# A selective scan with two PSUM banks for its inputs' products and one summing product per channel group

## The chip, the cores and the metric

The kernel runs on one core of a Trainium2 chip. A core has five engines that work side by side and meet at semaphores: PE (matrix products into PSUM), DVE (vector), ACT (activations), POOL (GpSimd) and SP, which here only issues DMAs. [...] The metric is the time of one execution on the device in microseconds.

## The reference

The input is x of shape (8, 512, 128): 8 sequences of 512 positions with 128 channels. Six layers are added to x in turn: an adapter FFN, attention, the same FFN, a mixture of experts, the selective scan, the same mixture. Only the scan layer is touched. It gets xn, the layer norm of x, and computes per sequence

```
u     = silu(conv3(xn))                    # depthwise, three taps along the positions
B, C  = split(u @ W_bc + b_bc)             # 16 numbers each per position
dt    = log1p(exp((u @ W_dt + b_dt) @ W_dtp + b_dtp))
alpha = exp(A * dt)                        # per channel d and state n, A = -exp(A_log)
beta  = B[n] * xn[d] * dt[d]
h[l]  = alpha[l] * h[l-1] + beta[l]        # the scan along the positions
y[d]  = sum over n of C[n] * h[d, n] + xn[d] * Dcoeff[d]
```

and x becomes x + y. 128 channels with 16 states each are 2048 recurrences of 512 steps.

## The kernel before

All of x stays in SBUF. The scan layer treats the sequences one after the other. The 2048 recurrences of one sequence are 16 groups of 8 channels x 16 states = 128 partitions, 512 positions in the free dimension.

Work is laid out by hand in steps and slots. A step (`over_steps`) treats three sequences at a time: `new`, whose dt, B and C are being made, `old`, whose 16 groups are scanned, and `older`, whose y is added to X; `ahead` is `new + 1`, whose convolution and projections are made. A step has 16 slots, `n` = 0 to 15. Each engine runs its own list of these slots in order, and within a slot in the order of the lines. An engine that waits for a semaphore holds up all that stands behind it on that engine.

For group m of `old` the work is:

- SP loads the 8 rows of dt, each 16 times, from DRAM into a ring buffer `dtb` (`load_dt`, L1598, 256 KB). It waits until ACT has used that buffer before. DT_RING is 4.
- ACT makes alpha from it in PSUM (`pA`, L1848). A_RING is 3: the write waits until scan m - 3 is over.
- PE spreads x * dt over the states from `stack` (three bf16 parts that add up to the value) into `pX` (`spread_xdt`, L1709), two slots ahead, in three banks.
- DVE multiplies pX with B into `beta` (L1891) and, one slot later, runs the scan into `h` (L1874).
- POOL multiplies h with C into `hc` (L1662), a ring of 8.
- PE sums over the states: `add_round` (L1724) takes four groups at a time in slots 6, 10, 14 and, for the last four, in slot 1 of the next step. Group 4r + t goes with a 32-column weight to PSUM partitions 32t to 32t + 31 of `pY`, into which the skip term x * D was written first (`skip_term`, L1717, four products of 32 columns). ACT copies the finished pY to yT (L1854).

The inputs of a sequence pass on PE through one PSUM bank `z`. `event` (L1671 to L1700) issues seven kinds of products into it: b and c (B and C spread over partitions, L1699, slots 2 and 3), y (four transposes back to rows, L1693, slot 4), xT (four transposes, L1682, slot 7), u (the convolution as three products with diagonal weights, L1686, slot 9), bc (two projections, L1689 and L1690, slot 12), lin (dt's second projection, L1696, slot 14). Each waits for its own input and until the one before it was read out of z. The readers are ACT, for b (L1828), c (L1831), xT (L1793), exp of u (L1796), the bias additions (L1804, L1805) and exp of dt (L1810), and DVE, for y (the addition to X, L1883, slot 5) and u (the product with 1/(1 + exp(-u)), called inv, L1868, slot 11).

dt and x * dt are then finished by ACT and POOL: w and its logarithm, nd, corr, dt, xdt (POOL L1631 to L1643, slots 1, 3, 4, 5), the three bf16 parts (ACT L1836 and L1839, POOL L1646 and L1649, slots 6 to 8). SP writes dt to DRAM in slot 6 and copies the parts into the stack in slot 10, 12 DMAs one after the other (L1590) once the third part is there; only then follow the next sequence's loads of dt.

PSUM has eight banks: pA 3, pX 3, pY 1, z 1.

Of the kernel before, what the change touches and what calls it, by code (L numbers as in the profile page):

```python
# [14 lines left out]
ALU = mybir.AluOpType  # L15
# [5 lines left out]
P = 128  # L21
# [1418 lines left out]
A_RING = 3  # L1440
X_RING = 3
DT_RING = 4
B_RING = 4
HC_RING = 8
LOW = 64
PARTS = 3
# [70 lines left out]
def selective_scan(nc, g, q, sem, tag):  # L1517
# [5 lines left out]
        "c_ready", "xdt_bcast", "alpha_ready", "beta", "h_ready", "hc_ready", "rounds", "y_taken", "y_done", "x_done",  # L1523
# [4 lines left out]
    with ExitStack() as ctx:  # L1528
# [9 lines left out]
        xT = [sb(f"xT{i}", [P, L + 2]) for i in range(2)]  # L1538
# [16 lines left out]
        z = ps("z", [P, L])  # L1555
        z3 = z[:, :].rearrange("p (c d) -> p c d", c=NC)
# [22 lines left out]
        def _(sp):  # L1579
# [4 lines left out]
            def stack_parts(b):  # L1584
                sp.wait_ge(s.split, b + 1)
                if b > 1:
                    sp.wait_ge(s.xdt_bcast, NS * (b - 1))
                for part in range(PARTS):
                    for t in range(TILES):
                        sp.dma_start(stack[b % 2][32 * part:32 * part + 32, t, :], parts[32 * t:32 * t + 32, part, :]  # L1590
                                     ).then_inc(stack_in[b % 2], 16)

            def load_dt(b, n):
                if n == 0:
                    sp.wait_ge(s.dt_out, 16 * (b + 1))
                wait_for(sp, s.alpha_ready, NS * b + n - DT_RING)
                first = channels(n)
                sp.dma_start(dtb[n % DT_RING][:, :],  # L1598
                             dt_dram[b % 2, first:first + DG, :].unsqueeze(1).broadcast_to([DG, NS, L])
                             ).then_inc(dt_in[n % DT_RING], 16)  # L1600

            def step(new, old, older):
                for n in range(NS):
                    if new is not None and n == 6:
                        write_dt(new)
                    if new is not None and n == 10:
                        stack_parts(new)
# [3 lines left out]
                    elif new is not None:  # L1611
                        load_dt(new, n + DT_RING - NS)

# [3 lines left out]
        def _(pool):  # L1617
            def zero_columns():
                pool.memset(xT[0][:, :], 0.0)
                pool.memset(xT[1][:, :], 0.0).then_inc(s.zeros_made, 1)  # L1620
# [7 lines left out]
            def inputs(b, n):  # L1628
# [3 lines left out]
                if n == 3:  # L1632
# [3 lines left out]
                if n == 4:  # L1636
# [4 lines left out]
                if n == 5:  # L1641
                    pool.wait_ge(s.dt_ready, b + 1)
                    pool.tensor_tensor(xdt[:, :], xT[b % 2][:, 1:L + 1], dt[:, :], ALU.mult).then_inc(s.xdt_ready, 1)  # L1643
# [7 lines left out]
            def step(new, old, older):  # L1651
                for n in range(NS):
                    if new is not None:
                        inputs(new, n)
                    if old is not None:
# [4 lines left out]
                        if m >= HC_RING:  # L1660
                            pool.wait_ge(s.rounds, m // TILES - 1)
# [6 lines left out]
        def _(pe):  # L1668
            pe.wait_ge(s.zeros_made, 1)

            def event(name, b, last):  # L1671

                need = {"xT": s.xn_ready, "u": s.xT_ready, "bc": s.us_ready, "lin": s.bc_ready, "b": s.bc_ready,
# [296 lines left out]
```

## Time and profile before

| | us |
|---|---|
| median of 3 executions | 1702.7 (1701.62 to 1707.16) |
| the profiled execution | 1707.51 |
| its span, first to last instruction | 1705.8 |
| PE busy in it | 1428.3 (84%) |
| DVE busy | 962.8 (56%) |
| ACT busy | 776.0 (45%) |
| POOL busy | 376.1 (22%) |

The profile's lines belong to one execution. An engine is busy while one of its instructions runs; matrix products are pipelined, so a busy PE is not PE at its peak. "Idle before" is the time that an engine stood still ahead of an instruction, and the arrow names what it waited for last. The scan layer runs from about 1016 us (its first instruction) to 1382 us, a little over a fifth of the span, and the shares above say little of it; windows and timelines of that stretch are read instead.

### The profile page before, as it was taken

Reading aid. Unit: us, or ns where it says so; the run is one execution under the profiler, and the core shown is the slowest. Engines: PE = TensorE matmul, PEld = TensorE weight load, DVE = VectorE, ACT = ScalarE, POOL = GpSimd, SP = SyncE. Lnnn points to the kernel's source line nnn. Section 1 sums busy time; section 2 is a strip of 40 time slices with the busy share of each in tenths; the row PEclk is TensorE's granted clock in tenths of the full one; section 3 lists DMA queues with packets and bytes.
Section 4 is the critical chain, followed back from the end, with each engine's and each line's share of the span. In section 5 each row is a group of like instructions: output and inputs, shape, how many; then the busy total and the mean of one; then the engine's idle time right before and its main releaser. Section 6 shows DMA issues by size and latency. Waiting matters only on the chain. (4 is left out here: it accounts for less than half of the span.)

```text
span 1705.8 us, 23654 instructions
## 1 busy us (share of the span) xinstructions
PE 1428.3 (84%) x7538; PEld 771.7 (45%) x7538; DVE 962.8 (56%) x1959; ACT 776.0 (45%) x1362; POOL 376.1 (22%) x475
## 2 busy tenths in 40 slices
PE   3983899999999688699999965777777559999998
PEld 2661223233322366567776741111111037777776
DVE  4663788888888166441222460777677864122235
ACT  0210488888888421154334323645554314433342
POOL 2004232321230100120000011666666630000000
PEclk9995799999999799599999986666766558999999
DMA  4002121222220000100000000433333410000001
GB/s 85 1 1 74 47 70 45 66 66 75 67 74 21 1 1 1 16 15 15 1 15 15 1 1 26 141 123 119 122 125 121 118 36 15 3 13 15 15 7 44
DMA packets 80052, 77.28 MB, mean 45 GB/s; under 512 B 19468, under 2 KB 59224, under 8 KB 79960
## 3 DMA queue, kind: packets, MB, share of 16 engines
q1 hardware_dynamic: 77840, 75.85, 14.6%
q8 instruction: 49, 0.80, 0.2%
q10 hardware_dynamic: 2120, 0.28, 0.1%
q14 instruction: 43, 0.35, 0.1%
HBM read 55.78 MB, written 16.78 MB: 43 GB/s over the span
## 5 line engine op out<-in xcount | busy, mean ns | idle before, releaser
L1258 ACT ACTIVATE m_hidden<-m_pU,m_up_b 128x512 f32<-128x512 f32 x320 | 219.9, 687 | 271.8 <-PE m_pU L1395 271.5
L1013 DVE TENSOR_REDUCE at_nm<-at_mx 128x2 f32<-128x1024 f32 x256 | 303.1, 1221 | 45.6 <-PE at_mx L857 44.3
L1402 PEld LDWEIGHTS m_pD<-m_down,m_hidden 128*128 128x128 f32 x2560 | 296.9, 192 | 33.5 <-issue 33.5
L1402 PE MATMUL m_pD<-m_down,m_hidden 128*128 128x128 f32 x2560 | 297.1, 275 | 0.0
L1395 PE MATMUL m_pU<-m_xT_all,m_up 128*128 128x512 f32 x640 | 291.3, 601 | 1.1 <-PEq L1094 1.1
L959 ACT ACTIVATE at_probs<-at_ring 128x512 f32<-128x512 f32 x512 | 268.3, 601 | 45.4 <-PE at_ring L869 44.6
L1371 DVE TENSOR_TENSOR m_out_b<-m_pD,m_down_b 128x512 f32<-128x512 f32 x64 | 44.2, 691 | 283.8 <-PE m_pD L1402 283.8
L1662 POOL TENSOR_TENSOR ss_hc<-ss_h,ss_c_all 128x512 f32<-128x512 f32 x128 | 161.0, 1267 | 113.2 <-DVE ss_h L1874 106.1
L857 PE MATMUL at_mx<-at_kk,at_qq 48*128 48x512 bf16 x512 | 158.3, 399 | 23.6 <-DMA at_kk<-k_stack 13.2
L1395 PEld LDWEIGHTS m_pU<-m_xT_all,m_up 128*128 128x128 f32 x640 | 118.0, 193 | 123.8 <-issue 123.5
L869 PE MATMUL at_ring<-at_qq,at_kk 51*128 51x512 bf16 x512 | 166.6, 386 | 8.0 <-ACT at_probs L959 4.9
L1874 DVE TENSOR_TENSOR_SCAN ss_h<-ss_pA,ss_beta 128x512 f32<-128x512 f32 x128 | 154.8, 1214 | 11.0 <-issue 4.4
L881 PE MATMUL at_po<-at_probs,at_va 128*32 128x512 f32 x1024 | 136.9, 607 | 0.1
L122 POOL TENSOR_TENSOR rstd<-ln_u,neghalf 128x4 f32<-128x4 f32 x6 | 6.1, 1023 | 552.2 <-DVE ln_u L114 552.2
L1709 PE MATMUL ss_pX<-ss_stack,ss_spread 96*128 96x512 bf16 x128 | 64.8, 522 | 67.4 <-DVE ss_beta L1891 62.1
L1848 ACT ACTIVATE ss_pA<-ss_dtb,ss_a_neg 128x512 f32<-128x512 f32 x128 | 87.1, 685 | 47.0 <-DMA ss_dtb<-ss_dt_rows 34.7
L857 PEld LDWEIGHTS at_mx<-at_kk,at_qq 48*128 48x128 bf16 x512 | 34.4, 95 | 131.7 <-DVE at_nm L1013 76.2
L1891 DVE TENSOR_TENSOR ss_beta<-ss_pX,ss_b_all 128x512 f32<-128x512 f32 x128 | 85.0, 669 | 5.9 <-PE ss_pX L1709 5.9
L1709 PEld LDWEIGHTS ss_pX<-ss_stack,ss_spread 96*128 96x128 bf16 x128 | 13.0, 106 | 161.8 <-DVE ss_beta L1891 113.6
L1377 DVE SCALAR_TENSOR_TENSOR m_acc<-m_out_b,m_w_listed,m_acc 128x128 f32<-128x128 f32 x256 | 73.2, 347 | 9.3 <-DVE m_out_b L1371 2.4
L869 PEld LDWEIGHTS at_ring<-at_qq,at_kk 51*128 51x128 bf16 x512 | 36.5, 93 | 63.7 <-ACT at_probs L959 42.3
L347 PE MATMUL f_pG<-f_hx 128*128 128x257 f32 x256 | 60.1, 387 | 5.2 <-ACT f_hx L386 5.2
(244 smaller groups left out, 1588.7 us busy)
## 6 DMA issues: line engine op xcount, KB each, us to landing
ss_dtb<-ss_dt_rows SPq DMA_DIRECT2D x128, 256.0 KB
at_qq<-q_stack SPq DMA_DIRECT2D x64, 96.0 KB, 2.3
at_kk<-k_stack SPq DMA_DIRECT2D x64, 96.0 KB, 2.3
q_stack<-at_qs SPq DMA_DIRECT2D x8, 384.0 KB, 2.6
k_stack<-at_ks SPq DMA_DIRECT2D x8, 384.0 KB, 3.0
ss_stack<-ss_parts SPq DMA_DIRECT2D x96, 32.0 KB, 1.9
X<-in_L_attn_x_dram SPq DMA_DIRECT2D x8, 256.0 KB, 5.6
q_stack<-at_qs SPq DMA_DIRECT2D x8, 256.0 KB, 2.9
```

The costliest lines, as they stand in the source:

```text
L857: last = pe.matmul(mx[parity][:, c, :], qq[rows(parity, STACK), pair, q_at:q_at + P], kk[rows(parity, STACK), pair, :], start=True, stop=True)
L869: pe.matmul(ring[bank][:, :], kk[rows(h, STACK + 3), h // 2, tile * P:(tile + 1) * P], qq[rows(h, STACK + 3), h // 2, :], start=True, stop ...
L881: last = pe.matmul(po[VW * h4:VW * (h4 + 1), :], va[:, tile, group * GH + h4, :], probs[:, (slot % 2) * GH + h4, :], start=(tile == 0), st ...
L959: act.activation(probs[:, (slot % 2) * GH + ORDER[j], :], ring[bank][:, :], ACT.Exp, scale=SCALE).then_inc(s.exp_done, 1)
L1013: dve.tensor_reduce(nm[group % 2][:, 2 * half:2 * half + 2, 2 * (pair % 2) + parity], mx[parity][:, :, :], AX.X, ALU.max, negate=True).the ...
L1258: act.activation(hidden[t % 2][:, k, :], pU[k][:, :], ACT.Gelu, bias=up_b[buf][:, k:k + 1]).then_inc(s.gelu_done, 1)
L1395: pe.matmul(pU[k][:, :], up[buf][:, k * P:(k + 1) * P], xT_all[:, t, :], start=True, stop=True).then_inc(s.up_done, 1)
L1402: last = pe.matmul(pD[t % 2][:, c, :], hidden[t % 2][:, k, c * P:(c + 1) * P], down[buf][:, k, :], start=(k == 0), stop=(k == NI - 1))
L1662: pool.tensor_tensor(hc[m % HC_RING][:, :], h[m % HC_RING][:, :], c_all[old % 2][:, :], ALU.mult).then_inc(s.hc_ready, 1)
L1848: act.activation(pA[m % A_RING][:, :], dtb[n % DT_RING][:, :], ACT.Exp, scale=a_neg[:, column:column + 1]).then_inc(s.alpha_ready, 1)
L1874: dve.tensor_tensor_scan(h[m % HC_RING][:, :], pA[m % A_RING][:, :], beta[m % B_RING][:, :], 0.0, ALU.mult, ALU.add).then_inc(s.h_ready, 1)
L1891: dve.tensor_tensor(beta[m % B_RING][:, :], pX[m % X_RING][:, :], b_all[old % 2][:, :], ALU.mult).then_inc(s.beta, 1)
```

## The change

- The bank z becomes two: `zx` holds xT and the convolution, `zy` holds y, b, c, the two projections and dt's second projection. pA gives up a bank for it: A_RING 3 to 2.
- `event` is replaced by functions with their own waits, and the slots are dealt out anew. On PE: xT of `ahead` in slot 1 (was 7), the convolution one product each in slots 3, 4, 5 (was 9), y in slot 4, b in 7 (was 2), c in 9 (was 3), the projections in 11 (was 12), lin in 13 (was 14). ACT, POOL, DVE and SP follow: the addition to X in slot 7 (was 5), the product with inv in 10 (was 11), POOL's corr, dt, xdt one slot earlier, the normalisation of x a step earlier and in two halves (slots 11 and 13).
- `add_round` becomes `add_group`: each group's states are summed by a product of its own, three slots after the group's place (groups 0, 1, 2 together in slot 5, 13, 14, 15 in slots 0, 1, 2 of the next step). `hc` buffers come free one by one.
- xT has three buffers instead of two, cleared by one memset more. dtb has six instead of four.
- SP writes dt in slot 4 (was 6), and the stack is copied in three parts in slots 7, 9 and 11, each as soon as its bf16 part is there (was all in slot 10).

```
-A_RING = 3
+A_RING = 2
-DT_RING = 4
+DT_RING = 6
+X_SEQS = 3
...
-        z = ps("z", [P, L])
+        zx, zy = ps("zx", [P, L]), ps("zy", [P, L])
...
-                    if new is not None and n == 6:
-                        write_dt(new)
-                    if new is not None and n == 10:
-                        stack_parts(new)
...
+                    if new is not None and n == 4:
+                        write_dt(new)
+                    if new is not None and n in (7, 9, 11):
+                        stack_part(new, (n - 7) // 2)
...
-                            pool.wait_ge(s.rounds, m // TILES - 1)
+                            pool.wait_ge(s.summed, m - HC_RING + 1)
...
+            def transpose_x(b):
+                pe.wait_ge(s.xn_ready, b + 1)
+                if b > 0:
+                    pe.wait_ge(s.us_ready, b)
...
+            def y_rows(b):
+                pe.wait_ge(s.y_taken, b + 1)
+                pe.wait_ge(s.e_dt, min(b + 3, NB))
...
+            def spread_b(b):
+                if b > 1:
+                    pe.wait_ge(s.x_done, b - 1)
+                pe.wait_ge(s.e_dt, b + 1)
...
+            def spread_c(b):
+                pe.wait_ge(s.b_ready, b + 1)
...
+            def project(b):
+                pe.wait_ge(s.us_ready, b + 1)
+                if b > 0:
+                    pe.wait_ge(s.c_ready, b)
...
-            def add_round(b, r):
-                wait_for(pe, s.hc_ready, NS * b + TILES * r + TILES - 1)
-                first = (ROUNDS - 1 - r) * DG
-                for t in range(TILES):
-                    ins = pe.matmul(pY[32 * t:32 * t + 32, :], q.total[:, first:first + 32],
-                                    hc[(TILES * r + t) % HC_RING][:, :], start=False, stop=(r == ROUNDS - 1),
-                                    skip_group_check=True)
-                ins.then_inc(s.rounds, 1)
+            def add_group(b, n):
+                wait_for(pe, s.hc_ready, NS * b + n)
+                tile = n % TILES
+                first = (ROUNDS - 1 - n // TILES) * DG
+                pe.matmul(pY[32 * tile:32 * tile + 32, :], q.total[:, first:first + 32], hc[(NS * b + n) % HC_RING][:, :],
+                          start=False, stop=(n // TILES == ROUNDS - 1), skip_group_check=True).then_inc(s.summed, 1)
...
+                    if n == 1 and ahead is not None:
+                        transpose_x(ahead)
+                    if n < 3 and older is not None:
+                        add_group(older, NS - 3 + n)
+                    if n in (3, 4, 5) and ahead is not None:
+                        convolve(ahead, n - 3)
                     if n == 4 and old is not None:
                         skip_term(old)
                     if n == 4 and older is not None:
+                        y_rows(older)
+                    if n > 4 and old is not None:
+                        for group in range(0 if n == 5 else n - 3, n - 2):
+                            add_group(old, group)
+                    if n == 7 and new is not None:
+                        spread_b(new)
+                    if n == 9 and new is not None:
+                        spread_c(new)
+                    if n == 11 and ahead is not None:
+                        project(ahead)
+                    if n == 13 and ahead is not None:
+                        lift(ahead)
```

ACT's list has the matching order: the copy of xT in slot 2, of pY in 3, the cast of xdt in 5, exp of the convolution in 6, the cast of rest and the logarithm in 7, inv in 8, the copies of b and c in 9 and 10, the bias additions in 12, exp of dt in 14, w in 15.

## Rows read from the trace of the kernel before

**Rows 1.** The page's part 2, 40 slices of the span.

```profile
PE   3983899999999688699999965777777559999998
...
PEclk9995799999999799599999986666766558999999
```

**Rows 2.** Windows from first scan to next; us, busy by engine, clock, DMA share, GB/s.

```profile
1068.70:1105.00 36.30, 26.49 (x68) 6.36 (x67) 28.23 (x33) 20.78 (x37) 26.58 (x22) 0.69 0.39 133
1105.00:1145.80 40.80, 30.21 (x80) 7.67 (x80) 29.86 (x40) 21.91 (x40) 27.06 (x23) 0.67 0.36 122
...
1346.80:1375.50 28.70, 16.40 (x57) 2.88 (x56) 27.88 (x37) 10.89 (x16) 18.98 (x16) 0.56 0.44 124
sum 306.80, PE 212.29 PEld 51.24 DVE 234.68 ACT 150.15 POOL 207.95; mean PE 26.54 PEld 6.40 DVE 29.34 ACT 18.77 POOL 25.99
```

**Rows 3.** Groups by line, 1030 to 1390; busy us, mean ns, idle before, releaser.

```profile
L1662 POOL TENSOR_TENSOR ss_hc<-ss_h,ss_c_all 128x512 f32<-128x512 f32 x128 | 161.0, 1267 | 113.2 <-DVE ss_h L1874 106.1 <-issue 7.0
L1874 DVE TENSOR_TENSOR_SCAN ss_h<-ss_pA,ss_beta 128x512 f32<-128x512 f32 x128 | 154.8, 1214 | 11.0 <-issue 4.4 <-DVE ss_beta L1891 3.6 <-ACT ss_pA L1848 2.9
...
L1891 DVE TENSOR_TENSOR ss_beta<-ss_pX,ss_b_all 128x512 f32<-128x512 f32 x128 | 85.0, 669 | 5.9 <-PE ss_pX L1709 5.9
...
L96 DVE BATCH_NORM_STATS2 bn<-X 128x6 f32<-128x128 f32 x32 | 6.9, 279 | 0.0
```

**Rows 4.** Timeline 1186.5 to 1200.5; start, us, engine, line, idle before and releaser.

```profile
1192.26 2.04 PE L1699 MATMUL ss_z<-ss_bc,ss_pick_bc 32*128 32x512 f32 x2 [0.23 <-ACT ss_b_all L1828]
...
1194.77 1.94 PE L1717 MATMUL ss_pY<-ss_xT,ss_diag_d 128*32 128x512 f32 x8
...
1196.63 0.93 PE L1693 MATMUL ss_z<-identf,ss_yT 128*128 128x128 f32 x4
...
1197.61 0.69 DVE L1883 TENSOR_TENSOR X<-X,ss_z 128x512 f32<-128x512 f32 x1 [4.65 <-PE ss_z L1693]
```

**Rows 5.** Timeline 1200 to 1219, what stands before the us product.

```profile
1203.59 0.62 ACT L1836 CAST ss_parts<-ss_xdt 128x512 bf16<-128x512 f32 x1 [5.93 <-POOL ss_xdt L1643]
...
1207.80 4.36 PE L1686 MATMUL ss_z<-ss_xT,ss_diag_k 128*128 128x512 f32 x6 [2.14 <-ACT ss_xT L1793]
...
1209.48 7.53 SPq L1590 DMA_DIRECT2D ss_stack<-ss_parts  x12
...
1212.19 0.60 ACT L1796 ACTIVATE ss_e<-ss_z 128x512 f32<-128x512 f32 x1 [3.34 <-PE ss_z L1686]
...
1214.61 0.69 DVE L1868 TENSOR_TENSOR ss_us<-ss_z,ss_inv 128x512 f32<-128x512 f32 x1 [4.45 <-ACT ss_inv L1801]
```

**Rows 6.** The same stretch, PE's products at full clock.

```profile
1211.99 0.38 PE L1709 MATMUL ss_pX<-ss_stack,ss_spread 96*128 96x512 bf16 x1
...
1212.30 1.07 PE L1724 MATMUL ss_pY<-ss_hc,ss_total 128*32 128x512 f32 x8
...
1213.30 0.39 PE L1709 MATMUL ss_pX<-ss_stack,ss_spread 96*128 96x512 bf16 x1
...
1216.28 1.04 PE L1689 MATMUL ss_z<-ss_us,ss_w_bc 128*32 128x512 f32 x2
```

**Rows 7.** Timeline 1022 to 1076, a 32-column product at half clock.

```profile
1061.16 1.89 PE L1689 MATMUL ss_z<-ss_us,ss_w_bc 128*32 128x512 f32 x2 [2.83 <-DVE ss_us L1868]
```

**Rows 8.** Windows of clock and DMA within the scan.

```profile
1187.10:1197.00 9.90, 9.67 (x25) 1.99 (x26) 5.85 (x7) 6.92 (x15) 8.62 (x7) 0.50 0.41 138
1197.20:1200.60 3.40, 1.27 (x9) 0.45 (x11) 2.96 (x8) 0.45 (x1) 0.00 (x0) 0.99 0.60 192
1200.70:1210.40 9.70, 6.30 (x18) 2.25 (x11) 8.94 (x11) 4.13 (x7) 9.34 (x8) 0.50 0.20 65
...
1220.00:1230.00 10.00, 6.93 (x24) 1.55 (x24) 10.00 (x13) 7.27 (x12) 7.70 (x8) 0.73 0.52 195
1348.00:1368.00 20.00, 12.81 (x47) 2.37 (x39) 19.19 (x27) 8.12 (x12) 13.06 (x11) 0.59 0.53 148
```

**Rows 9.** Timeline 1009 to 1024.5, the start of the scan.

```profile
1018.01 0.53 POOL L1620 MEMSET ss_xT<- 128x514 f32 x1
```

More of the change, by code:

```diff
@@ L1537, in selective_scan @@
         xn = sb("xn", [P, NC, D])
-        xT = [sb(f"xT{i}", [P, L + 2]) for i in range(2)]
+        xT = [sb(f"xT{i}", [P, L + 2]) for i in range(X_SEQS)]
         dt, xdt, rest = sb("dt", [P, L]), sb("xdt", [P, L]), sb("rest", [P, L])
@@ L1618, in zero_columns @@
             def zero_columns():
-                pool.memset(xT[0][:, :], 0.0)
-                pool.memset(xT[1][:, :], 0.0).then_inc(s.zeros_made, 1)
+                for i in range(X_SEQS):
+                    last = pool.memset(xT[i][:, :], 0.0)
+                last.then_inc(s.zeros_made, 1)
             take_rstd(pool, g, s.var, s.rstd, zero_columns)
@@ L1772, in _, with norm @@
             act.wait_ge(s.zeros_made, 1)
-            def norm(b):
-                act.wait_ge(s.rstd, NB)
-                act.wait_ge(s.shift, 2)
-                if b > 0:
-                    act.wait_ge(s.xT_done, b)
-                for c in range(NC):
+            def norm(b, half):
+                if half == 0:
+                    act.wait_ge(s.rstd, NB)
+                    act.wait_ge(s.shift, 2)
+                    if b > 0:
+                        act.wait_ge(s.xT_done, b)
+                for c in (2 * half, 2 * half + 1):
@@ L1851, in step @@
                         back(new, n)
-                    if n == 2 and older is not None:
-                        act.wait_ge(s.rounds, ROUNDS * older + ROUNDS)
+                    if n == 3 and older is not None:
+                        act.wait_ge(s.summed, NS * older + NS)
                         act.copy(yT[:, :], pY[:, :]).then_inc(s.y_taken, 1)
-                    if following(new) is not None:
-                        front(new + 1, n)
+                    if ahead is not None:
+                        front(ahead, n)
+                    if following(ahead) is not None and n in (11, 13):
+                        norm(ahead + 1, (n - 11) // 2)
+            for half in range(2):
+                norm(0, half)
             for n in range(NS):
+                if n == 4:
+                    for half in range(2):
+                        norm(1, half)
                 front(0, n)
```

181 lines of the change are left out of this document (79 added, 102 removed).

## The prediction, made before the changed kernel ran

> **What bounds the kernel now.** I read the page's slices first [rows 1]: the change touches only the scan, the stretch from about 1026 to 1382 us, and there the granted clock of TensorE sinks to 0.5 to 0.7 while PE is busy for 6 to 7 tenths. Then the windows from one sequence's first scan to the next one's [rows 2]. Eight of them make 306.8 us: 36.3, then six that make 241.8 (40.3 each), then 28.7 for the last sequence. In a middle one (40.8 us) DVE is busy for 29.86, POOL for 27.06, PE for 30.21 at a clock of 0.67, ACT for 21.91. No engine is full, so each waits for another in turn.
>
> The groups by line [rows 3] give the pieces: per channel group DVE does one product of 0.67 and one scan of 1.21 us, which overlap a little. 29.86 less the us product (0.69), the add to X (0.69) and the statistics (0.86 and a small copy) leaves 27.5, or 1.72 per group. POOL does 22 operations of about 1.26 per sequence, 27.1 busy. The floors are 29.8 (DVE) and 27.1 (POOL).
>
> What DVE waits for is seen in the order of time. One wait is the add to X [rows 4]: idle 4.65 us until the transposes of y into z are done. These stand in PE's order behind b, its copy, c, its copy and the skip term: all of them use the one bank z or stand between its users, and all run at half clock (2.04 for c, 1.94 for the skip term). The other is the us product [rows 5]: idle 4.45 until ACT has made inv. ACT sat 5.93 us before its cast of xdt (POOL's xdt comes late because POOL itself stood still while DVE waited for X), so it copied xT late, the three products of the convolution ran 1207.80 to 1212.16, and e, e1, inv followed. The two waits are 9.1 of the interval's 10 idle us. Both are latency in a chain, not a full engine.
>
> **The change part by part.** I count in slots, one per group, and in warm (full) clock unless said.
>
> *Two banks and the new places.* y's transposes now go to zy in slot 4 and the add to X stands in slot 7, three slots later (5 us). xT's transposes move from slot 7 to slot 1, the convolution from 9 to 3 to 5, e, e1, inv to 6, 7, 8, and the us product stands in slot 10. The b and c products move behind them (7 and 9). So the 4.65 and the 4.45 both go, if PE reaches slot 4 and 5 in time. Removed idle: 9.1 per middle interval at most, which would give 31.
>
> *Sum per group instead of rounds.* In [rows 6] a round, four products on 32 columns each, is issued as 8 passes and takes 1212.30 to 1213.30, 1.00 us for all four: they run side by side. A single product on 32 columns of the same 512 (L1689) takes 1.04 with its tail, so alone each costs what the round costs. Between any two of the new group products stands a spread product on all 128 columns, so they can't run together. Twelve products of 1.0 are added: +12 us of PE per sequence. A slot costs 0.31 (spread, 1211.99 to 1212.30) + 1.00 = 1.31.
> PE per sequence is then 16 x 1.31 = 21.0, the skip term 1.0, convolution 2.7 (half of what it takes cold, about 5.3), b and c 2.0, the two projections 2.0, dt 1.0, the two sets of transposes 1.0: 30.7 us warm. At half clock (one 32-column product 1.89 [rows 7], the rest doubled) it is about 58.
> [...]
>
> *Which clock.* [Rows 8]: PE was busy for 9.67 of 9.90 us at 0.50, and the next 3.4 us were granted 0.99; in these PE was busy for 1.27 only, and behind them stands 0.50 again. In [rows 1] the slices with PE at 9 have a clock of 9. With 30.7 of work in about 31.5, PE has no idle stretch of more than a microsecond, so I take full clock for the middle intervals. This is the largest choice in the forecast and is priced below.
>
> *The walk through one middle interval.* With the DVE slots at 0, 0.6, 2.3, 4.0, 5.7, 7.5, 9.2, 10.9, then the add to X, PE runs slots 0 to 3 by 5.5; slot 4 (spread, convolution, skip term, y) ends at 8.2, so y is there before DVE's slot 7 at 10.9: this wait is gone. Slot 5 (spread, convolution, three group sums) ends at 12.4, which DVE doesn't feel, since its next two spread products are already issued (three pX banks).
> POOL: hc of group 0 at 2.3, then nd, corr, dt, xdt between the hc's, xdt done at 12.2, rest at 15.8, the third part at 19.5.
> ACT is the tight one, since pA has two banks instead of three: the exponential of group n may begin only when scan n-2 is over, and is wanted 2.3 us later, 0.69 of them its own; so anything that ACT waits for behind exponential n has about 0.9 us to spare after slot n+1 has begun. Its cast of xdt in slot 5 comes at 12.2 and delays scan 6 by 0.5 (most of it is under the add to X). The cast of rest in slot 7 comes at 15.8 and delays scan 8 by 0.75. c's product waits for the copy of b and PE idles about 1 us there. The bias copies in slot 12 wait for the projections (25.3) and delay scan 13 by 0.55. dt in slot 14 just fits. Sum: 29.5 + 2.0 = 31.5, and PE arrives at the end of the same interval at 31.4. Queue overheads that I didn't walk: I add 0.5 and take 32.
> Bounds of the interval: 29.8 (DVE alone) and, if each of the four late handovers to ACT comes 1 us later, 35.5.
>
> *DMA.* Per sequence 16 loads of 256 KB, 12 of 32 KB and the 256 KB written, 4.85 MB. [Rows 8] show 195 GB/s in one dense stretch and 148 in the last sequence, at the same share (0.52, 0.53): 24.9 or 32.8 us. SP's own issuing is 12 in 7.53 us [rows 5] for the stack and about 0.6 for each load: 17.5 per sequence, so it is not full. On SP the write of dt now waits with loads 11 onward queued behind it, until POOL's dt at 9.7; six buffers instead of four cover that (load 11 is wanted at 21). The stack goes in three fours, the last behind loads for the next sequence, and lands near 28 for a use at 28.8: small margin, up to 1 us if missed.
>
> *The ends.* The third xT buffer is cleared on POOL between the two parts of rstd, for which ACT's first normalisation waits: 0.5 us [rows 9]. The step that fills the pipe keeps its chain at half clock; b and c stand later, the stack starts earlier: 0, within 2 either way. The interval of sequence 0 has neither y nor X: 30. That of sequence 6 has no convolution behind it: 30. The last sequence has DVE at 27.88 of 28.70 already [rows 2] and stays 28.7; after it the last sum is one product instead of four at the same time: 0.
> Sum: 30 + 5 x 32 + 30 + 28.7 = 248.7 against 306.8, and 0.5 for the memset: 57.6 us less. The profiled execution took 1707.5 us for a span of 1705.8 and would become 1649.9. It stands 4.8 above the median of the three runs shown, 1702.7, so I forecast 1645 for the median.
>
> **The rivals.**
> *The clock stays where it is (slower).* Mechanism: PE's waits for hc and for banks keep it from looking busy, the clock stays at 0.67 as in the middle intervals [rows 2], and PE now has 12 us more to do. A third of the time warm and two thirds cold gives 1/(0.34/30.7 + 0.66/58) = 44.5 per interval; with 30 for the last, 341 against 307: 35 us more, 1738. It decides below a mean granted clock of 0.75, where the interval is 40.3 as before. For it: PE was busy through 9.9 us before the clock rose [rows 8], and the low clock of the whole stage. Against: an engine with 12 us more work has no room for idle stretches like the one before that fall. [...]
> *ACT becomes the bound, through two pA banks.* 35.5 per middle interval and 33 for the two beside: 5 x 35.5 + 66 + 28.7 = 272, 35 less: 1668. For it: in the walk every remaining stall is of this kind. Against: after DVE's own delay ACT has caught up.
> *The loads.* At 148 GB/s throughout, 33 per interval: 7 x 33 + 30 = 261, 46 less: 1657. For it: the last sequence ran so from end to end. Against: dense stretches before it had 195.
> *The waits are not removed* because the two banks are held as long as the one was (zy still takes y, b, c, both projections and dt): the intervals stay near 39 and PE's extra work is hidden: 1697 to 1703, no change.
>
> **How the numbers follow.** Forecast with its own spread (1635 to 1652) 0.55; loads 0.12; ACT 0.18; no change 0.04; clock 0.08; better than the walk, to DVE's floor (28.2 + 5 x 29.8 + 29.4 + 27.9 = 234.5, 1630), 0.03. The range 1634 to 1670 leaves out the clock, no change and a little of the rest. A difference of 0.3% (5 us) is what a measurement of this kernel can tell from none. Faster 0.88, same 0.04, slower 0.08.
>
> **What would show it.** Right: from scan to scan 31 to 33 us, DVE busy over 90% of it, no wait of DVE for the transposes or inv over 1 us, PE's granted clock above 0.95 in the middle intervals, PE busy for over 28 us of each, single group sums about 1 us apart from their spread product. ACT's exponentials then wait for scans. Wrong: a clock below 0.75 there; or DVE's scans waiting for pA by several us per interval behind ACT's casts or bias copies; or ACT's exponentials waiting for dtb at a steady 1.77 us.

## The result, and the profile after

| | before | after |
|---|---|---|
| median | 1703.5 us (1701.62 to 1707.16, 4 executions) | 1642.34 us (1639.34 to 1647.64, 4 executions) |
| the profiled execution | 1707.51 | 1639.34 |
| its span | 1705.8 | 1637.6 |
| granted clock of TensorE, mean (1 is full speed) | 0.870 | 0.932 |

The ratio is 0.9642, 95% interval 0.9608 to 0.9676: the change makes the kernel 61 us faster. 1645 had been forecast, with a range of 1634 to 1670. The profiled execution of the kernel before is not one of the four in its median.

The page's slices of the span show where it happened; the rows answer to [rows 1].

```profile
PE   3893799999999869689999995699998769999998
PEclk9996699999999989769999998689999959999999
```

In the scan PE now stands at 9 in slices 27 to 30, and its clock at 8 or 9 in slices 27 to 32, where both had 5 to 7.

The same windows as [rows 2], from a sequence's first scan to the next one's (the first, three middle ones, the last, and the sum of all eight):

```profile
1061.80:1093.40 31.60, 28.18 (x66) 6.13 (x65) 28.48 (x34) 21.60 (x39) 27.08 (x22) 0.82 0.50 154
1093.40:1124.60 31.20, 30.19 (x84) 7.04 (x83) 30.01 (x41) 20.29 (x36) 26.90 (x22) 0.98 0.48 161
...
1156.20:1188.90 32.70, 30.52 (x82) 6.98 (x80) 29.93 (x40) 20.75 (x37) 27.02 (x23) 0.95 0.50 151
1188.90:1220.10 31.20, 27.39 (x79) 6.61 (x78) 29.93 (x41) 20.78 (x37) 27.12 (x23) 1.00 0.47 150
...
1281.10:1309.00 27.90, 22.21 (x61) 3.94 (x60) 27.82 (x37) 10.17 (x15) 19.17 (x16) 0.98 0.30 107
sum 247.20, PE 221.39 PEld 49.13 DVE 235.08 ACT 147.99 POOL 208.43; mean PE 27.67 PEld 6.14 DVE 29.39 ACT 18.50 POOL 26.05
```

The usual middle interval takes 31.2 us and not 40.8. DVE's work is what it was (29.93 against 29.86), so what went is its idle time, from 11 to 1.3 us. The waits of DVE in one middle interval, before (first fence) and after (second), show the same. The columns are: what waited for what, us in total, times, longest.

```profile
DVE ss_us L1868 <- ACT ss_inv L1801: 5.6, 1, 5.6
DVE X L1883 <- PE ss_z L1693: 4.8, 1, 4.8
DVE ss_h L1874 <- DVE ss_beta L1891: 0.5, 1, 0.5
```

```profile
DVE ss_h L1899 <- DVE ss_beta L1916: 1.2, 2, 1.0
```

Both named waits are gone and nothing of weight stands in their place. Lines from the timelines of PE, DVE and ACT in a middle interval, with the places of [rows 4 to 6]:

```profile
1188.06 1.05 PE L1739 MATMUL ss_pY<-ss_hc,ss_total 128*32 128x512 f32 x2
...
1189.03 0.39 PE L1724 MATMUL ss_pX<-ss_stack,ss_spread 96*128 96x512 bf16 x1
...
1196.99 1.06 PE L1739 MATMUL ss_pY<-ss_hc,ss_total 128*32 128x512 f32 x6
...
1198.62 0.66 DVE L1908 TENSOR_TENSOR X<-X,ss_zy 128x512 f32<-128x512 f32 x1
...
1200.16 0.62 ACT L1847 CAST ss_parts<-ss_xdt 128x512 bf16<-128x512 f32 x1 [4.10 <-POOL ss_xdt L1645]
...
1201.83 1.22 DVE L1899 TENSOR_TENSOR_SCAN ss_h<-ss_pA,ss_beta 128x512 f32<-128x512 f32 x1 [1.00 <-DVE ss_beta L1916]
...
1206.68 0.67 DVE L1893 TENSOR_TENSOR ss_us<-ss_zx,ss_inv 128x512 f32<-128x512 f32 x1
1207.15 1.12 PE L1704 MATMUL ss_zy<-ss_bc,ss_pick_bc 32*128 32x512 f32 x2 [1.05 <-ACT ss_b_all L1853]
...
1217.46 0.39 PE L1724 MATMUL ss_pX<-ss_stack,ss_spread 96*128 96x512 bf16 x1 [1.09 <-DMA ss_stack<-ss_parts]
```

The addition to X (1198.62) and the product with inv (1206.68) follow their predecessors at once. Most of the idle time that DVE has left stands at 1201.83: ACT sat 4.10 us before its cast of xdt, so the exponential behind it was late. The profile names beta there, which had ended a microsecond before; in new_xdt_early below, where the cast comes earlier, the wait is gone. c's product waits 1.05 for the copy of b and runs warm, which is to say at full clock (1.12 us at a granted 1.00; cold, at a granted 0.50, it took 2.04 in [rows 4]). The line at 1196.99 holds three group sums, x6 being two passes for each: with no spread product between them they took 1.06 us together.

The profiled spans differ by 68.2 us: 59.6 in the eight intervals (306.8 to 247.2), 3.5 in the step that fills the pipe, 1.35 between the last scan and the next layer's rstd, 0.3 behind the layer, and 3.4 ahead of it, in layers that the change doesn't touch.

### The profile page after: what moved, and what is told of

It reads as the page before. It is cut to its first block and busy times, and to the rows that moved or that the text cites. A ratio compares the mean times of both kernels' runs of the same rounds, so it can differ in the third digit from the quotient of the medians.

```text
span 1637.6 us, 23647 instructions
## 1 busy us (share of the span) xinstructions
PE 1433.1 (88%) x7538; PEld 767.2 (47%) x7538; DVE 962.8 (59%) x1959; ACT 775.8 (47%) x1362; POOL 377.0 (23%) x476
## 5 line engine op out<-in xcount | busy, mean ns | idle before, releaser
L1664 POOL TENSOR_TENSOR ss_hc<-ss_h,ss_c_all 128x512 f32<-128x512 f32 x128 | 161.9, 1271 | 50.6 <-DVE ss_h L1899 40.8
L1739 PE MATMUL ss_pY<-ss_hc,ss_total 128*32 128x512 f32 x256 | 122.5, 622 | 11.7 <-POOL ss_hc L1664 11.6
L857 PEld LDWEIGHTS at_mx<-at_kk,at_qq 48*128 48x128 bf16 x512 | 34.3, 95 | 131.4 <-DVE at_nm L1013 77.7
L869 PEld LDWEIGHTS at_ring<-at_qq,at_kk 51*128 51x128 bf16 x512 | 36.5, 93 | 64.1 <-ACT at_probs L959 42.4
```

What stands on the lines that cost most here:

```text
L857: last = pe.matmul(mx[parity][:, c, :], qq[rows(parity, STACK), pair, q_at:q_at + P], kk[rows(parity, STACK), pair, :], start=True, stop=True)
L869: pe.matmul(ring[bank][:, :], kk[rows(h, STACK + 3), h // 2, tile * P:(tile + 1) * P], qq[rows(h, STACK + 3), h // 2, :], start=True, stop ...
L1664: pool.tensor_tensor(hc[m % HC_RING][:, :], h[m % HC_RING][:, :], c_all[old % 2][:, :], ALU.mult).then_inc(s.hc_ready, 1)
L1739: pe.matmul(pY[32 * tile:32 * tile + 32, :], q.total[:, first:first + 32], hc[(NS * b + n) % HC_RING][:, :], start=False, stop=(n // TILES ...
```

## The experiments

The times are medians, and each ratio is to the kernel before on the same chip. Beside the experiments that kernel took 1706.5, 1707.0 and 1705.1 us, beside the new one 1703.5, so where two changed kernels are compared the difference of their ratios is the fairer measure. "Intervals" are the eight from first scan to first scan in the profiled execution; the kernels' line numbers shift by a few.

**The rounds of four in the new kernel** (new_rounds), the last of them in slot 2 of the next step.

```
...
-                    if n > 4 and old is not None:
-                        for group in range(0 if n == 5 else n - 3, n - 2):
-                            add_group(old, group)
+                    if n in (6, 10, 14) and old is not None:
+                        add_round(old, (n - 6) // 4)
...
```

> The changed kernel with only the summing put back: rounds of four products side by side in slots 6, 10, 14 and in slot 2 of the next step. Theory of places (the gain comes from where y and the convolution stand, in two banks; the group products cost 12 us of PE that nothing waits for): DVE still does not wait for y or inv, 31 to 33 us per middle interval, 1638 to 1650 us, while the granted clock sinks to 0.6 to 0.8 because PE has 12 us less to do. Theory of the clock (the group products are what makes it fast, since they keep PE at full clock): the interval goes back to 34 to 37 us, 1662 to 1685. Theory of PE's load (PE at 30 of 31 us is what bounds the interval now): 30 us per interval, 1630 to 1634.

Measured: 1659.05 (1658.71 to 1661.37), 0.9723 (0.9706 to 0.9739). This lies between the forecasts of the three theories. The group products are worth 17 of the 61 us by the medians and 14 by the ratios, with some 6 us of uncertainty. The page's clock alone doesn't say how; PE's timeline in a middle interval does, with one line of DVE's at its end:

```profile
1146.94 0.39 PE L1724 MATMUL ss_pX<-ss_stack,ss_spread 96*128 96x512 bf16 x1 [1.61 <-DVE ss_beta L1917]
...
1150.77 2.07 PE L1704 MATMUL ss_zy<-ss_bc,ss_pick_bc 32*128 32x512 f32 x2 [3.44 <-ACT ss_b_all L1854]
...
1153.31 1.94 PE L1739 MATMUL ss_pY<-ss_hc,ss_total 128*32 128x512 f32 x8
...
1155.71 1.92 PE L1711 MATMUL ss_zy<-ss_us,ss_w_bc 128*32 128x512 f32 x2
1157.56 1.75 PE L1712 MATMUL ss_zy<-ss_us,ss_w_dt 128*64 128x512 f32 x2
1159.25 0.61 PE L1724 MATMUL ss_pX<-ss_stack,ss_spread 96*128 96x512 bf16 x2
...
1159.68 0.69 DVE L1917 TENSOR_TENSOR ss_beta<-ss_pX,ss_b_all 128x512 f32<-128x512 f32 x1 [1.85 <-PE ss_pX L1724]
```

With no group sums to do, PE stands idle for 1.61 and 3.44 us while it waits for beta and for b's copy. Behind the second gap c's product, the round and the two projections run at half clock (granted 0.50, 0.50 and 0.53), 7.7 us for what takes about 4.3 warm, an estimate from the warm times in these traces (1.12, 1.06, 1.04 and 1.07). The spread product behind them is late: DVE's beta waits 1.85 us for it at 1159.68. The interval is 34.0, with a clock of 0.80. POOL never waited for a sum here, so hc buffers that come free one by one are not what the group products bring.

**A product per group in the old kernel** (old_groups): one bank and its own slots, with `add_group` in slots 5 to 15 and 0, 1, and POOL and ACT waiting for single groups.

```
...
-                    if n in (6, 10, 14) and old is not None:
-                        add_round(old, (n - 6) // 4)
+                    if n > 4 and old is not None:
+                        for group in range(0 if n == 5 else n - 3, n - 2):
+                            add_group(old, group)
...
```

> The kernel before with only the summing changed: a product per group, three slots behind the group, bank z and all other slots as before. Theory of places: the two waits of DVE stay, only shorter by what the full clock takes off the b, c, skip and convolution products before them (about 2 us at each): 36 to 38 us per middle interval, clock 0.85 to 1, 1672 to 1688. Theory of the clock: the whole gain is here, 32 to 33 us, 1645 to 1655. A third, that 12 us more on PE cost time in the old order: 42 or more, 1715 or more.

Measured: 1690.54 (1685.17 to 1694.88), 0.9903 (0.9874 to 0.9933), 2.5 above the range of the theory of places and nearest to it. PE's sums stand in 13 places per sequence instead of 4 (groups 0 to 2 and groups 14 and 15 stand together), 1.04 us each at full clock, and the old kernel is 16 us faster. Its clock rises to 0.91 to 0.96 in the middle intervals, the waits shrink (y 2.3 to 4.4, inv 3.3), and the intervals go to 36.5 to 39.0.

**Two banks in the old kernel** (old_two_banks): A_RING 2, zx for xT and u, zy for the rest, each product waiting for the last reader of its own bank, all slots as before.

```
...
                 pe.wait_ge(need, b + 1)
-                if last is not None:
+                z, z3, bank = (zx, zx3, 0) if name in ("xT", "u") else (zy, zy3, 1)
+                if last[bank] is not None:
...
```

> The kernel before with only the banks changed: xT and the convolution in one bank, the rest in another, pA with two banks, all slots and the rounds of four as before. Theory of places: y still stands behind b, its copy, c, its copy and the skip term, and inv behind ACT's cast of xdt; both waits stay at 4 to 5 us, 39 to 41 us per interval, 1695 to 1712. Theory of the banks (what DVE waited for was the single bank): both waits shrink, 34 to 36 us, 1655 to 1675.

Measured: 1705.78 (1701.89 to 1709.5, 10 executions), 0.9991 (0.9979 to 1.0004): nothing. DVE's waits in a middle interval:

```profile
DVE ss_us L1870 <- ACT ss_inv L1803: 5.4, 1, 5.4
DVE X L1885 <- PE ss_zy L1694: 4.8, 1, 4.8
```

They stand where they stood, as the theory of places had it. In the old slots the one bank is not what the products waited for, and giving up the third pA bank has no cost that shows.

**The old kernel with PE kept busy** (old_filled): each spread product issued four times over, nothing else.

```
+FILL = 4
...
-                pe.matmul(pX[m % X_RING][:, :], q.spread[:, n // TILES, :, :].rearrange("c d n -> c (d n)"),
...
+                for k in range(FILL):
+                    ins = pe.matmul(pX[m % X_RING][:, :], q.spread[:, n // TILES, :, :].rearrange("c d n -> c (d n)"),
...
```

> The kernel before with each spread product issued four times into the same bank instead of once (same result, 11 us more of PE per sequence at full clock, no new wait). It has the clock's part alone. Theory of places: clock 0.85 to 1, the two waits 2 to 3 us each instead of 4.5 to 5, 36 to 38 us per middle interval, 1672 to 1690. Theory of the clock: 32 to 34, 1645 to 1658. If the added products cost more than the clock gives back: over 1705.

Measured: 1685.17 (1680.0 to 1686.3), 0.9862 (0.984 to 0.9883). Work that nobody needs makes this kernel 21 us faster, at least as much as the group sums do. First a window of 36 us that runs from this kernel's second interval into its third, then the third interval of the kernel with the group products:

```profile
1105.00:1141.00 36.00, 30.20 (x127) 9.74 (x127) 29.16 (x39) 20.80 (x36) 26.40 (x22) 0.95 0.39 135
```

```profile
1142.00:1178.50 36.50, 29.22 (x81) 6.91 (x81) 30.00 (x40) 21.54 (x38) 27.07 (x23) 0.95 0.39 136
```

Both show a clock of 0.95 where [rows 2] have 0.67. The middle intervals of the filled kernel have 0.91 to 0.95 and take 36.7 to 39.8 us. The other thing that group sums could bring, hc buffers that come free one by one, nobody waited for: in [rows 3] POOL's idle time before hc is 106.1 us for scans and 7.0 of issue, none for a sum. So in the old kernel the group sums act as filling.

**The same filling in the new kernel with rounds** (new_rounds_filled).

> The changed kernel with rounds of four put back and each spread product issued four times: the group products' effect on the clock without the group products. If they help by the clock alone (theory): the granted clock is back at 0.95 or more, the intervals are 31 to 32 us and the time 1637 to 1646, as with the group products. If their own merit counts (each sum follows its hc at once, hc buffers come free one by one): it stays at 33.5 to 34, near 1655 to 1660.

Measured: 1663.4 (1661.05 to 1663.73), 0.9753 (0.9737 to 0.9769), slower than either forecast. The mean clock rose from 0.80 to 0.90 and the time did not fall (1659 without it), so a better mean clock is not by itself what the group products bring. PE's timeline shows where the filling missed:

```profile
1146.38 1.92 PE L1726 MATMUL ss_pX<-ss_stack,ss_spread 96*128 96x512 bf16 x8
1151.10 2.07 PE L1705 MATMUL ss_zy<-ss_bc,ss_pick_bc 32*128 32x512 f32 x2 [2.81 <-ACT ss_b_all L1857]
1153.11 1.89 PE L1726 MATMUL ss_pX<-ss_stack,ss_spread 96*128 96x512 bf16 x4
1154.92 1.94 PE L1742 MATMUL ss_pY<-ss_hc,ss_total 128*32 128x512 f32 x8
```

The gap before c's product is still 2.81 us, and half clock stands behind it, now with the filling to do as well. DVE's wait for pX is 2.4 to 2.7 us per middle interval, where it was 1.7 to 1.9 without the filling.

**Only the gap filled** (new_rounds_gap_filled): the spread products of slots 8 and 9 issued 8 and 11 times, the others once.

```
...
+                for k in range({10: 8, 11: 11}.get(n, 1)):
...
```

> The new kernel with the sums in rounds of four again, and two of the sixteen spread products issued 8 and 11 times over (slots 8 and 9), just ahead of c's product. With the rounds alone (1659) PE stood idle for 3.44 us there, waiting for b's copy, and then ran c's product (2.07), the round (1.94) and the projections (1.92, 1.75) at half clock. Filling the spread products all over the interval did not help (1663), but it left 2.8 us of idle in just this place and half clock behind it. Theory 'the sums per group matter because they fill this one gap': c's product, the round and the projections run at full clock, DVE's waits for pX (1.9 per interval) go to under 0.5, intervals about 31.5 to 32.5 us and the time 1640 to 1649. Rival 'rounds are late in themselves, since each waits for its fourth group and stands ahead of the spread products': the intervals stay near 34 and the time at 1657 to 1663.

Measured: 1649.95 (1644.6 to 1652.03), 0.9684 (0.9665 to 0.9704), 1 us above what the first theory gave and well below the rival's 1657. The window of one middle interval, DVE's waits in it, and PE behind the gap:

```profile
1124.00:1155.70 31.70, 27.14 (x99) 7.48 (x98) 29.73 (x40) 20.72 (x37) 27.01 (x23) 0.82 0.46 154
```

```profile
DVE ss_h L1902 <- DVE ss_beta L1919: 1.9, 3, 0.7
```

```profile
1142.23 1.12 PE L1704 MATMUL ss_zy<-ss_bc,ss_pick_bc 32*128 32x512 f32 x2 [1.29 <-ACT ss_b_all L1856]
...
1143.60 1.09 PE L1741 MATMUL ss_pY<-ss_hc,ss_total 128*32 128x512 f32 x8
...
1145.17 1.92 PE L1711 MATMUL ss_zy<-ss_us,ss_w_bc 128*32 128x512 f32 x2
```

c's product and the round are warm, the wait for pX is gone, and the interval is 31.7 at a mean clock of 0.82, lower than the 0.90 of the kernel that needed 34.3. So this one gap is worth about half of what the group products are: 9 of the 17 us by the medians, 7 of the 14 by the ratios, with some 4 us of uncertainty. The theory's full clock at the projections did not come (1.92). The other half is not taken apart: besides the cold projections, DVE waits 0.7 to 1.8 us for pX in the last three intervals (32.6, 31.8, 28.9 against 31.2, 29.8, 27.9 after).

**The addition to X two slots later in the old kernel** (old_late_add), one bank and rounds as before.

```
-                    if n == 5 and older is not None:
+                    if n == 7 and older is not None:
```

> The kernel before with DVE's addition to X in slot 7 instead of 5, nothing else. Theory of places, for the single bank: the wait for y shrinks by two slots (3.4 us), but the transposes of xT wait for that addition in the one bank and inv comes no earlier, so the wait for inv grows by as much: 1698 to 1710, no change. If each wait stood for itself: 3.4 us less per interval, 1680 to 1686.

Measured: 1673.42 (1672.31 to 1676.6), 0.9814 (0.9796 to 0.9833): half of the whole gain from one digit. My theory, no change, fell, and the time is 7 us below the lowest that independent waits gave. The window, DVE's waits, and the timeline of the same interval:

```profile
1138.24:1172.59 34.35, 24.43 (x81) 6.31 (x80) 30.13 (x40) 20.78 (x37) 27.16 (x23) 0.80 0.42 137
```

```profile
DVE ss_us L1868 <- ACT ss_inv L1801: 2.4, 1, 2.4
DVE X L1883 <- PE ss_z L1693: 1.0, 1, 1.0
```

```profile
1149.42 1.27 POOL L1643 TENSOR_TENSOR ss_xdt<-ss_xT,ss_dt 128x512 f32<-128x512 f32 x1
...
1150.72 0.62 ACT L1836 CAST ss_parts<-ss_xdt 128x512 bf16<-128x512 f32 x1 [1.52 <-POOL ss_xdt L1643]
...
1154.23 0.58 ACT L1793 COPY ss_xT<-ss_z 128x512 f32<-128x512 f32 x1
...
1154.95 2.81 PE L1686 MATMUL ss_z<-ss_xT,ss_diag_k 128*128 128x512 f32 x6 [1.21 <-ACT ss_xT L1793]
```

The wait for y falls from 4.8 to 1.0, as it would. But the wait for inv, which stood six slots behind the addition and now stands four, falls too, from 5.6 to 2.4 (to 2.4 in three of the middle intervals, to 3.9 and 4.2 in the others). In [rows 5] ACT sat 5.93 us before its cast of xdt; here it sits 1.52. While DVE waited for y it made no h, so POOL stood before its next hc with xdt queued behind, ACT stood before the cast with xT's copy queued behind, and PE's convolution was late and at least partly cold (4.36 there, granted 0.50 and then 0.83; 2.81 here, granted 1.00). So about 2 of the 5 us of the second wait came from the first, by the mean over the middle intervals.

**Both in one bank** (old_groups_late_add).

> The kernel before (one bank z, its own slots) with two changes alone: a product per group, and the addition to X in slot 7 and not 5. Apart they gave 1690.5 and 1673.4 against 1706. Theory: each takes part of the same waits (y: 4.7, and 2.3 to 4.4 with the group products; inv: 5.6, to 2.4 with the late addition and 3.3 with the group products), so together y goes to 0.5 or less and inv to 1 to 2.4; intervals 33 to 34.5, time 1656 to 1668. If that holds, more than half of the change's gain needs no second bank. Rival 'they add up in full': 1655 to 1659. Rival 'the late addition has it all': 1671 to 1675.

Measured: 1671.53 (1667.87 to 1675.31), 0.9814 (0.9791 to 0.9838), the same as with the late addition alone: the rival "the late addition has it all" was right. My own theory, 1656 to 1668, fell. The wait for y is gone in four of the intervals 2 to 6 and 1.0 in the other one, the third. The wait for inv stays at 3.3 to 3.4 (4.9 in the third), and the intervals take 34.2 to 34.8 (35.9):

```profile
DVE ss_us L1868 <- ACT ss_inv L1801: 3.3, 1, 3.3
```

So half of the gain needs neither the second bank nor the group products. What is left is the wait for inv, and the new slots start the convolution earlier. No run has these slots with one bank, and as they are laid out they need two: zx is held from the convolution in slot 3 until the product with inv in slot 10, and y, b and c pass through zy meanwhile.

**The addition to X back in slot 5 of the new kernel** (new_add_early).

> The new kernel with the addition to X back in slot 5. By the walk y's transposes end about 8.2 us after the first beta, and DVE's slot 5 begins at 7.5 to 9: the wait for y would be 0 to 1 us, and since the old kernel showed that a wait of DVE there is passed on to POOL and ACT, up to 2 us more. Theory 'with the two banks y is early and the place of the addition is nearly free': intervals 31 to 32.5, 1641 to 1651. Rival 'the place of the addition is what counts in the new kernel too': intervals 33 and more, 1655 or more.

Measured: 1647.66 (1641.3 to 1649.65), 0.9655 (0.9625 to 0.9684), 5 us above the new kernel by the medians and 2 by the ratios, whose intervals overlap: as the first theory had it. The waits for y are 0.7 to 0.8 in four of the middle intervals, and these take 31.2 to 32.8 as without the edit. The other one, the second of the eight intervals, had a wait of 2.6 and took 36.3 us in the profiled execution; why only that one is not settled. With y's transposes done early the place hardly matters: it is the same digit that was worth 33 us in the old kernel.

**SP as before in the new kernel** (new_sp_as_before): all 12 stack DMAs in slot 11, four dtb buffers. The write of dt stays in slot 4.

```
-                    if new is not None and n in (7, 9, 11):
-                        stack_part(new, (n - 7) // 2)
+                    if new is not None and n == 11:
+                        for part in range(PARTS):
+                            stack_part(new, part)
...
-DT_RING = 6
+DT_RING = 4
```

> The new kernel with the stack copied in one piece in slot 11 (12 DMAs one after the other, once the third part is there) and four dt buffers instead of six. Theory: the last stack DMA is then issued about 7.5 us after slot 11's start (19.5 to 27.5) and lands 2 to 3 us later, near 30 and not 29.7 at most, for a use at 28.8; the loads behind it start later, and with four buffers ACT's exponentials wait for dtb in some slots. Intervals 32 to 34, time 1645 to 1660. Rival 'the three stack parts and the six buffers do nothing': 1640 to 1644.

Measured: 1662.47 (1660.73 to 1665.16), 0.9755 (0.9733 to 0.9777), 2 us above the forecast. Lines from a timeline of all engines, around the end of a middle interval:

```profile
1223.80 7.78 SPq L1590 DMA_DIRECT2D ss_stack<-ss_parts  x12
...
1232.87 0.39 PE L1725 MATMUL ss_pX<-ss_stack,ss_spread 96*128 96x512 bf16 x1 [3.27 <-DMA ss_stack<-ss_parts]
...
1235.77 0.69 ACT L1867 ACTIVATE ss_pA<-ss_dtb,ss_a_neg 128x512 f32<-128x512 f32 x1 [4.32 <-DMA ss_dtb<-ss_dt_rows]
1236.55 1.22 DVE L1900 TENSOR_TENSOR_SCAN ss_h<-ss_pA,ss_beta 128x512 f32<-128x512 f32 x1 [0.80 <-ACT ss_pA L1867]
```

SP's 12 issues take 7.78 us in one piece. The spread product waits 3.27 for them and ACT 4.32 for the loads of dt queued behind. In the kernel before, with five middle intervals of some 40 us, PE waited for no stack copy in them and ACT for the loads 1.7 us or less in each; here the intervals take 33.9 to 34.5 and 19 to 20 of the 61 us are lost. The earlier stack and the deeper ring were not told apart.

**POOL's dt chain one slot earlier** (new_xdt_early), at the stall that the new kernel has left: nd, corr, dt, xdt in slots 0 to 3, and not 1 to 4.

> The changed kernel with POOL's nd, corr, dt and xdt each one slot earlier (slots 0 to 3): POOL was idle for 1.1 us ahead of group 0's hc, and the cast of xdt on ACT, 4.1 us late, holds up an exponential and by it a scan by 1.0 us per interval. Theory of places (what is left of DVE's idle time is ACT behind POOL's xdt chain): DVE's idle time falls from 1.2 to 0.3 us, 30.2 to 30.6 us per interval, 5 to 8 us less, 1634 to 1638 beside 1642. Theory of PE's load (PE busy for 30 of 31.2 bounds it): no change, the wait moves to the spread products.

Measured: 1634.02 (1631.29 to 1636.58), 0.9587 (0.9572 to 0.9601), the best of all, 8 us below the new kernel by the medians and 9 by the ratios, as the theory of places had it. One middle interval:

```profile
1121.30:1151.30 30.00, 29.08 (x83) 6.92 (x82) 29.73 (x40) 20.72 (x37) 27.03 (x23) 1.00 0.55 168
```

DVE is busy for 29.73 of 30.00: four of the five middle intervals take 30.1 and are bound by DVE's own work. The fifth took 31.7, with a wait of 1.0 for pA and of 0.5 for pX.

**The third stack part earlier as well** (new_early_both): in slot 9, right behind the second.

> As new_xdt_early, and the third part of the stack is issued right behind the second, before the loads for the next sequence (PE waited 1.1 us for the stack in most intervals, but spread products are issued two slots ahead). Theory of places: another 0 to 3 us in all, since only intervals where the stack came more than 2 us late lose time there (one of 32.8 us). Theory of PE's load: the 1.1 us of PE per interval count in full, 6 to 8 us less than new_xdt_early.

Measured: 1638.09 (1635.18 to 1638.56), 0.9601 (0.9586 to 0.9616), no better than without it. DVE had nothing left to wait for in four of the five middle intervals, and the fifth took 31.7 as before, with the same two waits.

## Why the prediction was right

*The two waits go: right, in size too.* 9.1 of idle time were to go and a middle interval was to take 32, walked at 31.5. They took 31.2 to 32.7. The 9.1 were read in the interval where the waits were shortest; in the other middle intervals they make 9.9 to 10.4 (4.8 and 5.1 to 5.6). The walk's marks held: counted from the first beta (1187.74), xdt is there at 12.4 (walked 12.2) and PE's gap before c is 1.05 (about 1).

*A group product by itself costs 1.0 us: right. Twelve more of them: wrong.* A single one takes 1.05 with its tail, starts 0.32 after its spread product, and the next spread product starts 0.97 later. But no spread product stands between groups 0, 1 and 2, which share slot 5, and they took 1.06 together (1196.99). The sums stand in 14 places instead of 4, so 10 us were added and not 12. Slot 5 ended at 10.3 and not at the walked 12.4. PE was to be busy 30.7 us per middle interval at full clock; in new_early_both, where three such intervals in a row show 28.38, it was 2.3 less. The new kernel's 27.4 to 30.5 hold cold products, and a few records may be missing from the lowest. DVE didn't wait for slot 5, so the mistake changed no term of the interval's sum.

*The clock: right in the value, too simple in the reason.* The middle intervals were granted 0.95 to 1.00, though PE had more room to idle than the sum said. In two of the five, both at 0.95, a stretch at half clock remained; in the one of 32.7 us it came 1.3 us after the end of c's product, which again had waited 1.05:

```profile
1174.38 1.12 PE L1704 MATMUL ss_zy<-ss_bc,ss_pick_bc 32*128 32x512 f32 x2 [1.05 <-ACT ss_b_all L1853]
...
1177.30 1.92 PE L1739 MATMUL ss_pY<-ss_hc,ss_total 128*32 128x512 f32 x2
```

The argument also took the clock as one number. The gap-filled kernel has 0.82 and 31.7 us, the filled one 0.90 and 34.3: what counts in these two is whether the products on the chain behind a gap run cold.

*Stalls behind ACT: two of three came.* Scans 6, 8 and 13 were to lose 0.5, 0.75 and 0.55. In the interval shown scan 6 lost 1.00 and scan 8 0.20, and there is none at 13 (the one of 32.7 has a wait of 1.0 for pA and one of 0.5 for pX).

*The stack lands near 28: missed by 1.7.* It landed 29.7 after the first beta, and PE waited 1.09 us for it, though DVE did not. The 32 KB copies took 3.0 us from issue to landing (median), where the kernel before had 1.9. The last of the twelve was issued at 25.5 and took 4.2; at the old median of 1.9 it would have landed at 27.4, which is an estimate.

*The ends: off; the kernel gained more there than the sum had.* The fill step was put at 0, with 0.5 lost to the memset, and gained 3.5 in all. Of its two projections to dt (lin in the kernel), the first ran warm (1.12 against 2.04), as these rows of before and after show:

```profile
1040.66 2.04 PE L1696 MATMUL ss_z<-ss_dt_low,ss_w_dtp 64*128 64x512 f32 x2 [1.55 <-ACT ss_bc L1805]
```

```profile
1037.71 1.12 PE L1716 MATMUL ss_zy<-ss_dt_low,ss_w_dtp 64*128 64x512 f32 x2 [1.46 <-ACT ss_bc L1822]
```

Of the 3.5, 1.5 came before the first beta and 2.0 between it and the first scan (3.6 before, 1.6 after); what else made them up is open. The tail was put at 0 and gained 1.35, since the last sum is one warm product (1.04) and not a cold round, and y's transposes behind it run warm too (0.66 against 1.11):

```profile
1376.99 1.93 PE L1724 MATMUL ss_pY<-ss_hc,ss_total 128*32 128x512 f32 x8 [4.42 <-POOL ss_hc L1662]
```

The intervals were 247.2 and not 248.7. With the 3.4 ahead of the layer, which the change doesn't touch, this makes the profiled execution 10.6 us shorter than the 1649.9 worked out for it. The median is off by 2.7 only: the forecast took off the 4.8 by which before's profiled execution stood above the median then known, and after's profiled execution was its fastest, 3.0 below its median. So part of the closeness is luck.

*What the prediction had seen and not priced.* It says that POOL stood still while DVE waited for X, that xdt came late by this, and behind it xT's copy, the convolution and inv. That is the link that old_late_add shows. But it priced the two waits as two items that add up to 9.1, each removed by its own new place, and drew no forecast from the link; the expectation for old_late_add denied it and fell. It also gave no part of the gain to a single item: the second bank, which the change is named for, does nothing alone, the late addition alone gives half, and the group products give 14 to 17 us. Walking all parts together needed none of these shares. Forecasts of single parts held for the banks, the filling and the early addition, missed by 1 to 3 us for the group products in the old kernel, the filled gap and SP's order, and by more for the rounds in the new kernel and the late addition.

The rivals: the clock that stays low did not come true, but what it feared is seen in new_rounds: 3.44 us of idle, then the round at 1.94. Within one interval c's product and the round run there at half clock (2.07, 1.94) between rounds at full clock (1.06, 1.07), at a mean clock of 0.80. The new kernel shows it too, in two of its middle intervals, with gaps of 1.05 to 1.08 and a mean clock of 0.95. ACT as bound, through two pA banks, fell with old_two_banks and with the 30.1 us intervals of new_xdt_early, which has two pA banks as well. The loads: whole middle intervals ran at 150 to 168 GB/s, so 148 was no limit. Waits that stay, with the banks held as long as the one was, is what old_two_banks shows for the banks alone; with the new slots it did not happen.

## What to carry to other kernels

Before two waits in one interval are priced apart, follow who stands still because of the first: an engine that waits also holds up those that need its next result, and all that stands behind in their lists (ACT sat 5.93 us before its cast of xdt, and 1.52 once DVE's first wait was short). Moving one instruction two slots later was worth more here than a bank (33 us, the banks alone nothing). Read the clock at the products behind a gap, not as a mean: work put into that gap paid here even where nobody needed it (9 us, at a mean clock of 0.82). Sums on separate groups of 32 columns ran side by side here wherever no other product stood between them (three in 1.06 us, one in 1.05), so go through the order slot by slot before counting them. Once the intervals had shrunk by nearly a quarter, transfers that had been hidden (the 12 issues in one piece, or the loads behind them) came to the surface here (waits of 3.27 and 4.32 us), so look at them in the same change.

## What the runs showed of the hardware

- Issuing each spread product four times over, with nothing else changed, made a kernel 1.4% faster (0.984 to 0.9883); the granted clock of its middle intervals was 0.91 to 0.95, against 0.66 to 0.72 without.
- Idle times of 3.44 and 2.81 us before c's product were followed by half clock. After one of 1.29 us the next products were warm (1.12, 1.09), yet 3 us later the projection ran cold (1.92). After gaps of 1.05 us in the new kernel all that followed was warm in one interval (1207.15), and in another a sum 3 us later ran cold (1.92 at 1177.30). The runs don't show a rule for this.
- A sum on 32 columns alone took 1.04 to 1.05 us, three on different columns one right behind the other 1.06, four 1.00 to 1.07.
- A 32 KB copy from SBUF to SBUF took a median of 3.0 us from issue to landing with the stack in three parts between loads, and 1.9 in one piece, both before and in new_sp_as_before.
